# Two state-space stages of a four-layer network: another placement of the next sequence's front steps among the sixteen states of the running one

## The reference

```python
# L0_attn; L2_attn does the same with a LayerNorm in front and another layout of names
xn = x * rsqrt(mean(x * x, -1) + EPS) * norm_w
u, res = split(xn @ in_proj_w, 2)                        # 256 channels each
u = silu(sum(conv_w[:, k] * u_pad[:, k:k + L, :] for k in range(4)) + conv_b)
dt, Bm, Cm = split(u @ x_proj_w, [8, 8 + 16])            # 16 states
delta = softplus(dt @ dt_proj_w + dt_proj_b)
# per token t, for each of 256 channels and 16 states:
h = exp(delta_t * A) * h + (delta_t * u_t) * B_t
y = sum over states of h * C_t
out = ((y + u * D) * silu(res)) @ out_proj_w
```

## The kernel before, in words

| engine | norm | turn | in | tap 0, 1, 2, 3 | silus | dbc | dt |
|---|---|---|---|---|---|---|---|
| PE | 0 | 4 | 5 | 5, 6, 6, 7 | 7 | 8 | 9 |
| ACT | 4 | 6 | 7 | nothing to do | 9 | 10 | 11 |
| DVE | 0 | nothing to do | nothing | nothing | nothing | nothing | 13 |
| POOL | 2 | nothing | nothing | nothing | nothing | nothing | nothing |

## Time and profile before

### The profile page before, as it was taken

The page is one execution under the profiler, slowest core; times in us unless marked ns, Lnnn a source line. Parts: engine busy times, 40 slices in busy tenths (PEclk is TensorE's granted clock), DMA queues, the critical chain, the costliest instruction groups (busy, mean ns, idle before and its releaser), DMA issues. The chain is left out here.

```text
span 8349.2 us, 242917 instructions
## 1 busy us (share of the span) xinstructions
PE 6762.5 (81%) x92794; PEld 4774.9 (57%) x92858; DVE 5586.3 (67%) x11830; ACT 4966.7 (59%) x10684; POOL 4192.9 (50%) x3724
## 2 busy tenths in 40 slices
PE   5777999999999999999999679997888757644367
PEld 2324666666666666666666478885555423222245
DVE  6895777677677677677677557775667668853432
ACT  5545777778777777777777534444767655412022
POOL 4555666666666566666666335554444345522000
PEclk9888999999999999999999789998999878866578
DMA  3221111111111111111111110000000032233001
GB/s 127 112 109 51 40 39 52 39 38 49 41 39 50 41 42 46 44 39 38 52 38 41 45 44 5 5 6 26 17 22 16 13 143 109 114 115 79 22 0 30
DMA packets 234600, 413.43 MB, mean 50 GB/s; under 512 B 42120, under 2 KB 125792, under 8 KB 214560
## 3 DMA queue, kind: packets, MB, share of 16 engines
q1 hardware_dynamic: 225776, 377.91, 14.3%
q10 hardware_dynamic: 1584, 15.21, 0.5%
q0 software_dynamic: 6144, 5.25, 0.4%
HBM read 208.77 MB, written 32.18 MB: 29 GB/s over the span
## 5 line engine op out<-in xcount | busy, mean ns | idle before, releaser
L769 POOL TENSOR_TENSOR L0f_qr<-L0f_qs,L0f_table 128x512 f32<-128x512 f32 x776 | 989.7, 1275 | 456.9 <-ACT L0f_qs L810 353.0
L1024 PE MATMUL L0f_ring<-L0f_wqkv,L0f_hT 128*128 128x512 f32 x2324 | 1173.0, 610 | 42.2 <-ACT L0f_hT L805 37.5
L776 POOL TENSOR_TENSOR L0f_qr<-L0f_qr,L0f_m 128x512 f32<-128x512 f32 x776 | 985.2, 1270 | 162.2 <-issue 106.6
L840 ACT ACTIVATE L0f_scores<-L0f_scores,L0f_nmx,L0f_rn 128x64 f32<-128x64 f32 x3072 | 985.6, 401 | 131.2 <-DVE L0f_nmx L945 130.1
L1081 PEld LDWEIGHTS L0f_o<-L0f_pT,L0f_vmix 64*64 64x64 f32 x18480 | 759.3, 136 | 157.0 <-issue 134.1
L1081 PE MATMUL L0f_o<-L0f_pT,L0f_vmix 64*64 64x32 f32 x18480 | 801.6, 221 | 47.3 <-ACT L0f_pT L848 31.6
L1081 PE MATMUL L0f_o<-L0f_pT,L0f_vb 64*64 64x32 f32 x6160 | 750.8, 220 | 0.9 <-issue 0.7
L783 POOL TENSOR_TENSOR L0f_qr<-L0f_qr,L0f_rn 128x512 f32<-128x512 f32 x388 | 396.3, 1042 | 688.1 <-DVE L0f_rn L937 686.8
L914 DVE TENSOR_TENSOR L0f_m<-L0f_ring,L0f_table 128x512 f32<-128x512 f32 x776 | 524.2, 686 | 253.7 <-ACT L0f_qs L810 244.9
L1081 PEld LDWEIGHTS L0f_o<-L0f_pT,L0f_vb 64*64 64x64 f32 x6160 | 604.2, 137 | 0.9 <-issue 0.9
L922 DVE TENSOR_REDUCE L0f_ssq<-L0f_sq 128x8 f32<-128x512 f32 x776 | 509.8, 676 | 76.9 <-ACT L0f_sq L815 72.0
(11 more groups left out here) (540 smaller groups left out, 17013.4 us busy)
## 6 DMA issues: line engine op xcount, KB each, us to landing
L0f_vmix<-L0f_vb SPq DMA_DIRECT2D x768, 128.0 KB, 2.4
L0a_bc_all<-L0a_bc_rows SPq DMA_DIRECT2D x32, 2048.0 KB, 11.4
L2a_bc_all<-L2a_bc_rows SPq DMA_DIRECT2D x32, 2048.0 KB, 11.4
L0f_vmix<-L0f_vb SPq DMA_DIRECT2D x672, 64.0 KB, 2.0
L1f_vmix<-L1f_vb SPq DMA_DIRECT2D x96, 128.0 KB, 2.4
L0f_wqkv<-L_ffn_wqkv_dram SPq DMA_DIRECT2D x7, 1536.0 KB, 6.0
L2f_parts<-L2f_zero ACTq DMA_DIRECT2D x8, 1088.0 KB, 11.5
n_s<-mixer_out SPq DMA_DIRECT2D x32, 256.0 KB, 5.2
```

Source lines behind the costliest of these rows:

```text
L769: e.tensor_tensor(rotated, qs[:, q % QN], spread(cos, 1, 8), ALU.mult).then_inc(cosed.sem, 1)
L776: e.tensor_tensor(rotated, rotated, m2[:, q % SN], ALU.add).then_inc(added.sem, 1)
L840: a = e.activation(s_ps[:, s, h, j], s_ps[:, s, h, j], ACT.Exp, bias=nmx[:, s, col:col + 1], scale=rn[:, tt, 2 * u, col:col + 1])
L1024: e.matmul(bank[:], hT[:, tt * P:tt * P + P], wqkv[:, layer % 2, col:col + 512], start=True, stop=True).then_inc(full, 1)
```

## The change

The change touches the placements alone, and cuts the ACT part of `dt` in two: v, Abs and Exp stay in `dt`, and the Ln becomes a step `log` of its own, with the drain that stood ahead of it. No engine issues another instruction of arithmetic or another transfer than before.

```diff
-             [("silus",), ("dbc",), ("dt",)])
+             [("silus",), ("dbc",), ("dt",), ("log",)])
...
-        place.update({("tap", i): turn + 1 + (i + 1) // 2 for i in range(2 * D2)})
+        place.update({("tap", i): turn + 2 + i for i in range(2 * D2)})
...
# POOL
-            sequences(e, front, back, after_state(norm=2, turn=3, silus=7, dbc=8, dt=11))
+            sequences(e, front, back, after_state(norm=2, turn=3, silus=7, dbc=8, dt=11, log=11))
...
# ACT
                     e.activation(ln1[:], ln1[:], ACT.Exp, scale=-1.0)
+                    return
+                if kind == "log":
                     e.drain()
                     e.activation(ln1[:], ln1[:], ACT.Ln, bias=1.0).then_inc(logged.sem, 1)
...
-            sequences(e, front, back, after_state(norm=4, turn=6, silus=9, dbc=10, dt=11))
+            sequences(e, front, back, after_state(norm=3, turn=5, silus=10, dbc=11, dt=12, log=13))
...
# DVE
-            sequences(e, front, back, after_state(norm=0, turn=3, silus=7, dbc=8, dt=13))
+            sequences(e, front, back, after_state(norm=0, turn=3, silus=7, dbc=8, dt=14, log=14))
...
# PE
-            sequences(e, front, back, after_state(norm=0, turn=4, silus=7, dbc=8, dt=9), gated=0, result=0)
+            sequences(e, front, back, after_state(norm=0, turn=3, silus=9, dbc=10, dt=11, log=11), gated=0, result=0)
```

More of the change, by code:

```diff
@@ L1942, in mamba_net, with after_state @@
     FRONT = ([("norm",), ("turn",)] + [("in", c) for c in range(D2)] + [("tap", i) for i in range(2 * D2)] +
-             [("silus",), ("dbc",), ("dt",)])
-    def after_state(norm, turn, silus, dbc, dt):
-        place = {("norm",): norm, ("turn",): turn, ("silus",): silus, ("dbc",): dbc, ("dt",): dt}
+             [("silus",), ("dbc",), ("dt",), ("log",)])
+    def after_state(norm, turn, silus, dbc, dt, log):
+        place = {("norm",): norm, ("turn",): turn, ("silus",): silus, ("dbc",): dbc, ("dt",): dt, ("log",): log}
         place.update({("in", c): turn + 1 for c in range(D2)})
-        place.update({("tap", i): turn + 1 + (i + 1) // 2 for i in range(2 * D2)})
+        place.update({("tap", i): turn + 2 + i for i in range(2 * D2)})
         return [[s for s in FRONT if place[s] == n] for n in NS]
@@ L2259, in front @@
             def front(b, par, kind, key=None):
-                if kind == "norm":
+                if kind in ("norm", "log"):
                     return
```

## The result

| | before | changed |
|---|---|---|
| median us, 4 runs each | 8362.42 (8354.17 to 8378.82) | 8308.85 (8296.86 to 8309.45) |
| profiled execution's span | 8349.2 | 8306.6 |

The ratio is 0.993, 95% interval 0.9912 to 0.9948: faster by 43 to 74 us, 54 by the medians. Forecast were 68 us and 8296.5; the measured 8308.85 lies in the range. Timed a second time beside other runs of the kernel before, it came to 0.9918 (0.9905 to 0.9932), 69 us of 8378.

What follows compares the result with a forecast made beforehand. DVE sets the pace, held up by ACT's chain of inserted front work. The walk through one sequence cut excess from 8.22 to 3.34 us; 14 x 4.88 = 68 us off 8364.65 gives 8296.5 us, range 8274 to 8326.

Steps and rivals of the forecast that it cites:

- Step 1: Taps one per state: PE holds 3.43 us per state; the 2.38 us wait for the convolution's second half goes.
- Step 2: Silus behind ACT's state 10, gate matmuls behind PE's state 9: ACT's gap 5.98 us, before 8.20.
- Steps 3 and 4: ACT's gaps at dbc behind state 11, 0.82 us, and at dt without the Ln behind 12, 4.55 us.
- Step 5: Log behind ACT's state 13: gap 3.71 us as before, a table switch costing 1.30 us.
- Step 6: Norm, turn and in one state earlier: cost nothing; without the cover PE would be late by tenths.
- Step 7: DVE's delta and du behind state 14 instead of 13: same work, 2.8 us, covered with 2 us over.
- the named signs of being wrong: ACT's Silu gap over 7 us; PE's adds holding DVE; `bc_all` or du wait at next state 0; clock below 1.00.
- Step 8: SP's transfers start at dbc's eviction: 15.0 us of work in 17.9 us, covered with 2.9 over.
- the slower case: PE becomes the bound in states 4 to 11 at a mean clock below 0.73; 8603 us at 0.5; 4%.
- the shorter chain: ACT's waits of 0.7 us for v and 0.2 for dbc vanish: 13 us more gain, 8284 us; 4%.
- lost at the next state 0: Late du delays the next sequence by the 4.9 us won, so no change; 3%.
- PE's remaining backlog: PE enters state 4 with a backlog, so the 2.38 us wait remains: 33 us given back, 8330 us; 10%.

Runs made afterwards that it cites:

- Variant 4: Changed kernel with the old tap spacing on PE, behind states 4, 5, 5, 6 instead of 5, 6, 7, 8; ratio 0.9935.
- variant 2: Kernel before with only ACT's Ln split off, one state later (12); ratio 0.9954.
- variant 6: Changed kernel with DVE's delta and du back behind state 13 instead of 14; ratio 0.9899.
- variant 7: Changed kernel with PE's and ACT's front steps up to dbc one state earlier, ACT's Ln at 14; ratio 0.9874.
- experiment 1: Kernel before and changed kernel run once more, no edit; changed to before ratio 0.9918.
- variant 3: Changed kernel with the Ln back in the gap of v, Abs and Exp (ACT dt 12, log 12); ratio 0.9945.
- variant 8: Changed kernel with only ACT's dt and Ln later, at 13 and 15 instead of 12 and 13; median 8261.1 us, ratio 0.9868.

## Why the prediction was right, and where it was off

1. **What bounds.** Right, but for one word: the prediction puts all of DVE's waits in states 8 to 12, and a few of the 33 waits for adds stand in state 2 at the start of a sequence (one of 1.01 us at 305.11). They lie outside the walk and are there in both kernels. The gap theory (ACT's inserted work, less 5.33 us and 2.13 for each further gap) gave the stages of five of the seven variants beforehand within 3 us; the other two are 4 and 7, where PE was late and they were 1 to 6 us dearer.
2. **Step 1, the taps.** Right that PE holds 3.43 us per state at full clock: its rows in the changed kernel follow each other at 1.71 to 1.72 us from 164.64 to 178.38, and the second half is there when ACT asks. Variant 4 shows that this does not hang on the even spacing.
3. **Step 2, the Silus.** Right to the hundredth, 5.98 us. Both matmuls of the gate were ready as worked out (4.55 and 5.40 us behind t; forecast 4.55 and 5.41).
4. **Steps 3 and 4 are where the forecast was off.** The walk gave each pair of matmuls on PE 1.72 us also from the gate to dt. The PE timeline of the changed kernel:

```profile
183.08 1.88 PE L2312 MATMUL L0a_y<-L0a_hc,const_ident 128*128 128x512 f32 x4
184.89 1.91 PE L2304 MATMUL L0a_ring<-L0a_uc,L0a_w_x 128*40 128x512 f32 x4
186.74 1.98 PE L2312 MATMUL L0a_y<-L0a_hc,const_ident 128*128 128x512 f32 x4
188.65 1.98 PE L2287 MATMUL L0a_ring<-L0a_dbc,L0a_w_dt 8*128 8x512 f32 x4
```

   The pairs start 1.81, 1.85 and 1.91 us apart, and the first of them 1.82 behind the gate's (181.26). dt came 0.51 us later than worked out (t = 177.88; 10.77 instead of 10.26), so v's wait was 1.13 and not 0.7. Gaps 0.91 and 4.89 in place of 0.82 and 4.55, sum 15.51 in place of 15.06, excess 3.78 in place of 3.34: 0.44 us per sequence, 6 us of the 68. The trace of before had it: its dbc started at 257.39 and the adds behind it 1.84 later:

```profile
259.23 1.98 PE L2310 MATMUL L0a_y<-L0a_hc,const_ident 128*128 128x512 f32 x4
```

   The 0.82 also holds a slip: in the earlier trace rows the next pair starts 0.49 us behind the start of the eviction and not 0.60, which makes it 0.71 by the walk's own times. As v is held by PE, the next gap is longer by the same 0.11, and the sum stays.
5. **Step 5, the log.** 3.73 against 3.71. A switch of tables cost 1.31 us from the end of the last Exp to the Silu (179.21 to 180.52). The Trainium skill ("ScalarE: Activation LUTs", What ACT_TABLE_LOAD costs) adds a drain of 1.38 us to each switch; this trace does not agree, its load starts 0.02 us behind the Exp and the Silu 0.01 behind the load. The 2.13 us of the fourth gap are confirmed alone by variant 2.
6. **Step 6.** ACT's norm, turn and in cost nothing seen.
7. **Step 7, costed at nothing, was not.** It is true that no wait of DVE, which sets the pace, is for du at the new place. POOL and ACT do wait for it ahead of the next state 0 (4.41 us of ACT's idle time at 205.52), so one of the named signs of being wrong did appear, but it lies under DVE's own work. The step asks only whether the later place hurts and not what the earlier one would have filled: variant 6 wins 9 to 11 us a stage by leaving delta and du where they were. The sum is not off by this, since the wait of 1.58 us at state 14 is in it; the forecast priced the wait and missed that it could be filled.
8. **Step 8.** No row of the waits names a late quarter of B and C.
9. **The rivals.** The clock read 1.00 in the full states, so the slower case did not come; the shorter chain went the other way, with waits of 0.41 us for dbc and 1.13 for v that did not vanish. Nothing was lost at the next state 0: DVE waits there for some 2.0 us twice in a stage, as before. The stretch of the full states, with the columns of the earlier trace rows:

```profile
160.00:192.00 32.00, 30.94 (x74) 12.45 (x72) 31.41 (x38) 19.49 (x29) 22.95 (x20) 1.00 0.06 19
```

   PE's remaining backlog did not cost at the Silus: PE stood 0.34 to 1.01 us for ACT ahead of the gate's matmuls in each of the seven fronts of L0a. In variant 7, one state earlier, five of the seven had no such cover left.

Of the 14 us between 68 and the first measured 54, 2.3 lie in the stages; the others lie in the scatter of the rest. The timing of experiment 1 came to 69. The stages won 32.9 us where 7 x (8.22 - 3.78) is 31.1. The 1.8 us lie outside the span of states that was walked, and most of them in `delta`, whose pair of instructions was 0.24 us shorter behind state 14 than behind 13. Before, and changed:

```profile
206.64 1.52 DVE L2212 SCALAR_TENSOR_TENSOR L0a_delta<-L0a_v,L0a_ln 128x512 f32<-128x512 f32 x2
...
202.76 1.28 DVE L2214 SCALAR_TENSOR_TENSOR L0a_delta<-L0a_v,L0a_ln 128x512 f32<-128x512 f32 x2
```

The scans around it start 6.23 us apart before and 6.01 in the changed kernel, in every sequence of L0a, which makes 1.6 us a stage. Variant 6 has 1.51 us again at 13. Behind 13 a product of POOL still runs when the pair starts, behind 14 POOL stands idle and waits for du; that this is the reason was not tried apart. Luck had a small part: of the 3.1 us a stage that steps 3 and 4 gave away, this term, which the prediction does not count, returned 1.6.

## What to carry to other kernels

Where an engine serves a faster loop with a few buffers of lead, work slipped into its queue costs only what exceeds the lead, and each period between two pieces gives its idle time back; so cut a long piece at any dependence and leave whole periods between the halves, before looking for less work. The same sum tells which of two waits is real: the wait for PE was covered by ACT's, and where it was gone (variant 3) ACT's row rose by 6.4 us although the stage became shorter. An engine filled to its period is safe only as long as it enters on time (variant 7), and work of the bounding engine itself belongs where that engine would stand anyway (variant 6).

## What was not expected of the hardware

A pair of f32 matmuls of 512 columns starts 1.72 us behind the last pair through the adds and taps, and 1.81 to 1.91 around the pairs with 40 columns or 8 rows of weights. That the shape is the cause was not tried apart. And DVE loses about 2.0 us twice in a stage ahead of the scans of a state 0, in the kernel before as in the changed one (up to 2.8 in variant 8). In the changed kernel's timeline it reads

```profile
277.47 2.34 DVE L2226 TENSOR_TENSOR_SCAN L0a_da<-L0a_da,L0a_dbu 128x512 f32<-128x512 f32 x2 [1.99 <-POOL L0a_dbu L2106]
```

though POOL had begun the product at 272.31. It comes behind the third and the fifth sequence, which is where the loop of two sequences an iteration jumps back; in the kernel before, the same place bears 2.00 us with no releaser. That it is the jump itself was not tried. Last, in variant 8 the table load that leads back to Exp stood behind ACT's wait for du, not ahead of it, so that its 1.28 us come after a wait of 2.94:

```profile
197.06 1.28 ACT L2181 ACT_TABLE_LOAD   x1 [2.94 <-DVE L0a_du L2217]
```
